# A graph layer on one core: the edge pipeline one step deeper, and the node stage's last addition at the end of its step

## The reference

```python
h = maximum(layernorm(x), 0)
em = concat([h[src], h[dst]]) @ msg_w + msg_b           # 25,000 x 256 times 256 x 128
em = relu(layer_norm(em) * msg_g + msg_beta) * edge_weight[:, None]
messages = segment_sum(em, dst) / count(dst)            # mean over the edges of each target
gate = sigmoid(h @ gate_w + gate_b)
h_new = relu(layer_norm(concat([h, messages]) @ upd_w + upd_b) * upd_g + upd_beta)
out = x + gate * h_new + (1 - gate) * h
```

## Time and profile before

| | |
|---|---|
| median of 3 runs | 1020.86 us (1020.46 to 1021.62) |
| profiled execution, its own time | 1019.86 us |
| its span | 1017.1 us |
| busy in the span | DVE 945.0 us (93%), ACT 875.1 (86%), PE 705.2 (69%), POOL 680.7 (67%) |
| mean granted clock of PE | 0.776 of full speed |
| preparation and first node groups | 0 to 40 us |
| node loop and its end | to about 480 us |
| edge steps enter | from 481.52 us |
| last output scatter of POOL | 1005.43 us |

### The profile page before, as it was taken

How to read it: one execution, slowest core, us unless ns; L and a number is a source line. 1 busy time by engine, 2 the same in 40 slices (tenths; PEclk the granted TensorE clock), 3 DMA queues, 4 the chain that set the end, 5 groups by cost and what they waited for, 6 DMA issues and landing times.

```text
span 1017.1 us, 20909 instructions
## 1 busy us (share of the span) xinstructions
PE 705.2 (69%) x3696; PEld 547.4 (54%) x3696; DVE 945.0 (93%) x4103; ACT 875.1 (86%) x3664; POOL 680.7 (67%) x602
## 2 busy tenths in 40 slices
PE   1877776777777777777477767676867676666740
PEld 1555554555555555555366556565656565555530
DVE  6999999999999999999869999998998999999990
ACT  2899999999999999999778988888788897888860
POOL 5788888888888888100344777776776777677564
PEclk9999996555555555555578998989798989999975
DMA  4255555555555455332121222221212122121110
GB/s 142 79 153 149 154 152 151 151 154 151 149 155 153 148 153 155 113 115 82 52 82 59 62 73 65 68 70 58 68 61 70 56 68 70 55 68 60 55 58 21
DMA packets 56028, 100.65 MB, mean 99 GB/s; under 512 B 13728, under 2 KB 15600, under 8 KB 55948
## 3 DMA queue, kind: packets, MB, share of 16 engines
q1 hardware_dynamic: 35766, 64.54, 17.6%
q0 software_dynamic: 18912, 34.84, 14.4%
q10 hardware_dynamic: 1270, 0.53, 0.3%
HBM read 52.34 MB, written 51.45 MB: 102 GB/s over the span
## 4 chain that ended last, share of the span: by engine, by line
DVE 56%; issue 18%; ACT 12%; PE 4%; DVEq 4%; POOL 3%; DMA 1%; ACTq 0%; SPq 0%; POOLq 0%
DVE work L430 11%; DVE st L344 9%; DVE work L441 8%; ACT junk L393 5%; DVE work L447 5%; DVE acc L441 5%; DVE acc L885 4%; PE pa L1056 3%; POOL out L557 3%; DVE mv L350 3%; DVE work L452 2%; DVEq L109 1%; DVE gt L423 1%; DVE omg L426 1%; ACT hrow L386 1%
## 5 line engine op out<-in xcount | busy, mean ns | idle before, releaser
L552 POOL DMA_INDIRECT ring<-in_x,src_i x196 | 228.7, 1167 | 175.8 <-ACT hrow L386 110.1
L552 POOL DMA_INDIRECT ring<-in_x,gidx x196 | 237.7, 1213 | 59.7 <-issue 59.7
L557 POOL DMA_INDIRECT out<-work,sidx x196 | 209.8, 1071 | 88.5 <-issue 56.9
L1056 PE MATMUL pt<-ident,hrow 128*128 128x128 f32 x588 | 143.4, 391 | 116.8 <-ACT hrow L386 108.5
L1093 PE MATMUL py<-w_u,work 128*128 128x129 f32 x784 | 203.8, 441 | 0.0
L409 ACT ACTIVATE work<-work,gt 128x128 f32<-128x128 f32 x589 | 199.6, 403 | 2.6 <-DVE work L447 2.6
L1093 PEld LDWEIGHTS py<-w_u,work 128*128 128x128 f32 x784 | 174.9, 328 | 40.4 <-issue 40.4
L1056 PEld LDWEIGHTS pt<-ident,hrow 128*128 128x128 f32 x588 | 96.6, 197 | 145.9 <-ACT hrow L386 136.6
L386 ACT ACTIVATE hrow<-xload,nb,rs 128x128 f32<-128x128 f32 x392 | 161.6, 484 | 14.4 <-DVE nb L379 7.5
L441 DVE SCALAR_TENSOR_TENSOR work<-py,rs,g_upd 128x128 f32<-128x128 f32 x588 | 163.4, 339 | 4.2 <-ACT rs L373 4.2
L393 ACT ACTIVATE junk<-py 128x128 bf16<-128x128 f32 x588 | 150.5, 266 | 8.7 <-PE py L1131 7.8
(11 more groups left out here) (151 smaller groups left out, 1543.4 us busy)
## 6 DMA issues: line engine op xcount, KB each, us to landing
xload<-in_x SPq DMA_DIRECT2D x98, 256.0 KB, 3.3
out<-work SPq DMA_DIRECT2D x98, 256.0 KB, 2.0
running_sums<-acc SPq DMA_DIRECT2D x49, 256.0 KB
ring<-in_x,src_i POOLq DMA_INDIRECT x196, 3.2
ring<-in_x,gidx POOLq DMA_INDIRECT x196, 3.2
out<-work,sidx POOLq DMA_INDIRECT x196, 2.3
w_all<-in_L_gnn_msg_w ACTq DMA_DIRECT2D x1, 128.0 KB
w_all<-in_L_gnn_upd_w ACTq DMA_DIRECT2D x1, 128.0 KB
```

Of the source, the lines that this page charges most:

```text
L552: pool.indirect_dma_start(out=dest, out_offset=None, in_=rows, in_offset=bass.IndirectOffsetOnAxis(ap=idx, axis=0), **(if_tail if rows is ...
L557: pool.indirect_dma_start(out=out, out_offset=bass.IndirectOffsetOnAxis(ap=idx, axis=0), in_=rows, in_offset=None, **if_tail).then_inc(s, 16)
L1056: last = nc.tensor.transpose(dest[:, k * H:(k + 1) * H], rows[:, k, :], ident[:, :])
```

## The change

The edge pipeline becomes one step deeper behind the running sums. On PE the transposes of the sums are those of s-5 and stand first in the step; the update matmuls are those of s-5. On ACT the copy at is that of s-5 and stands between ht_dst and the relus; post, relus and the waits belonging to them go one group further back; ht_dst waits besides for the update matmuls of the group four before, since its buffer is now still read that late. On DVE gate, mix and update normalization are those of s-7, final that of s-9, and the update normalization (with its wait for the scatter) stands behind the message normalization rather than at the step's end. In the node stage final takes the group six back and stands at the end of the step, where it took the group seven back in the middle. The edge loops run one step more, the node loop of DVE one less. REFILLED is 36 in place of 40.

PE's order, edge steps ahead of the loop, before the change: from a message matmul to the first update matmuls (pm messages, pa sums, pt h, py update).

The diff, cut to its core:

```diff
@@ -52,7 +52,7 @@
 AHEAD = 8
-REFILLED = 40
+REFILLED = 36
 EPS = 1e-5
@@ -646,9 +646,6 @@
                     minus_mean(dve, nd, s.back(1), G)
-                f = s.back(7)
-                if live(f, NG):
-                    final(dve, nc.vector, nd, f, o[:, f.at % 4])
                 if new:
@@ -669,6 +666,9 @@
                     beta(dve, nd, g, t_buf[:, g.at % 4], be_upd)
+                f = s.back(6)
+                if live(f, NG):
+                    final(dve, nc.vector, nd, f, o[:, f.at % 4])
@@ -823,7 +823,7 @@
             def edge_step(s):
-                g, m = s.back(6), s.back(4)
+                g, m = s.back(7), s.back(4)
                 fin, new, summing = live(g, EG), live(s, EG), live(m, EG)
@@ -845,7 +845,7 @@
                     minus_mean(dve, ed, s.back(1), 2 * G, -0.5)
-                f = s.back(8)
+                f = s.back(9)
                 if live(f, EG):
@@ -855,6 +855,14 @@
                     beta(dve, ed, q, acc[:, q.at % 4], be_msg, G, "beta_m", "gamma_m")
+                if fin:
+                    if beyond(g, 4):
+                        dve.wait_ge(s_scat[g.at % 4], g.rounds(16 * G))
+                    else:
+                        dve.wait_ge(s_st[g.at], 16 * len(range(g.at, NG, 4)))
+                    ed["rstd"].after(dve, s)
+                    one_mark(ed["gamma"], dve, g, by_std(t_buf[:, g.at % 4], py[:, g.at % 2], s.at % 4, 3 * G, g_upd))
+                    beta(dve, ed, g, t_buf[:, g.at % 4], be_upd)
                 if new:
@@ -867,10 +875,6 @@
                 if fin:
-                    if beyond(g, 4):
-                        dve.wait_ge(s_scat[g.at % 4], g.rounds(16 * G))
-                    else:
-                        dve.wait_ge(s_st[g.at], 16 * len(range(g.at, NG, 4)))
                     ed["gain"].after(dve, g)
@@ -895,13 +899,8 @@
                     moment(L, s, 2 * G, 2)
-                if fin:
-                    ed["rstd"].after(dve, s)
-                    one_mark(ed["gamma"], dve, g, by_std(t_buf[:, g.at % 4], py[:, g.at % 2], s.at % 4, 3 * G, g_upd))
-                if fin:
-                    beta(dve, ed, g, t_buf[:, g.at % 4], be_upd)
-
-            run_steps(dve, node_step, NG, 7, 9, 8, first=4, beside=edge_step)
+
+            run_steps(dve, node_step, NG, 6, 9, 8, first=4, beside=edge_step)
@@ -920,7 +919,7 @@
-            run_steps(dve, edge_step, EG, 8, 2 * EUN, EUN, first=7, beside=tail_step)
+            run_steps(dve, edge_step, EG, 9, 2 * EUN, EUN, first=6, beside=tail_step)
@@ -983,8 +982,8 @@
                     ed["stats"].after(act, s.back(1))
-                if live(s.back(6), EG):
-                    ed["post"].after(act, s.back(6))
+                if live(s.back(7), EG):
+                    ed["post"].after(act, s.back(7))
                 if live(s.back(3), EG):
@@ -994,11 +993,16 @@
                 if live(g, EG):
+                    if beyond(g, 4):
+                        ed["upd"].after(act, g.back(4))
                     one_mark(ed["ht"], act, g, nc.scalar.activation(ht_dst[:, (g.at + NG) % 4, :], pt[:, 1, :], ACT.Copy))
-                if live(s.back(7), EG):
-                    gated_relu(act, ed, s.back(7))
-                if live(s.back(5), EG):
-                    post(act, ed, s.back(5), (s.at + 1) % 4, 3 * G, G, 1.0)
+                g = s.back(5)
+                if live(g, EG):
+                    evacuate(ed, g, at_[:, g.at % 2, :], pa[:, :], ACT.Copy, "at", "aflip")
+                if live(s.back(8), EG):
+                    gated_relu(act, ed, s.back(8))
+                if live(s.back(6), EG):
+                    post(act, ed, s.back(6), (s.at + 1) % 4, 3 * G, G, 1.0)
                 g = s.back(1)
@@ -1008,9 +1012,6 @@
                     H_.mark(h_rows(g, h_dst[:, (g.at + NG) % XS], slot(g, 1, at), G))
-                g = s.back(4)
-                if live(g, EG):
-                    evacuate(ed, g, at_[:, g.at % 2, :], pa[:, :], ACT.Copy, "at", "aflip")
                 if live(s.back(2), EG):
@@ -1035,7 +1036,7 @@
-            run_steps(act, edge_step, EG, 7, 2 * EUN, EUN, first=6, beside=tail_step)
+            run_steps(act, edge_step, EG, 8, 2 * EUN, EUN, first=6, beside=tail_step)
@@ -1095,6 +1096,10 @@
             def edge_step(s):
+                g = s.back(5)
+                if live(g, EG):
+                    ed["sum"].after(pe, g)
+                    one_mark(ed["aflip"], pe, g, flip(pa[:, :], acc[:, g.at % 4]))
                 g = s.back(2)
@@ -1107,16 +1112,12 @@
                     one_mark(ed["msg"], pe, g, last)
-                g = s.back(4)
-                if live(g, EG):
-                    ed["sum"].after(pe, g)
-                    one_mark(ed["aflip"], pe, g, flip(pa[:, :], acc[:, g.at % 4]))
                 g = s.back(1)
...
                     one_mark(ed["flip"], pe, g, flip(pt[:, 1, :], h_dst[:, (g.at + NG) % XS]))
-                g = s.back(4)
+                g = s.back(5)
                 if live(g, EG):
@@ -1137,7 +1138,7 @@
             run_steps(pe, node_step, NG, 2, 9, 8, first=2, beside=edge_step)
-            run_steps(pe, edge_step, EG, 4, 2 * EUN, EUN, first=2)
+            run_steps(pe, edge_step, EG, 5, 2 * EUN, EUN, first=2)
```

## The result

The changed kernel takes **1113.62 us** (median of 4 runs, 1112.67 to 1114.7) beside 1021.09 us before (1020.46 to 1021.62): ratio 1.0907, 95% interval 1.0888 to 1.0926. Slower, as forecast, but by 92 us instead of 52, and outside the range (1024 to 1095).

The account below looks back on a forecast made before the run. DVE bounds the kernel now; a new edge-stage ring would take over at 10.9 us per step. 41 steps +45.1, stops +4, passage -3, end +5.7 make +51.8, 1071.7 us; with 1.0 for the median, 1073 us, range 1024 to 1095.

Parts of the forecast that it names:

- The ring: Edge stage: a new circle of waits between PE and ACT sets the step, 9.81 us at full clock against 9.52.
- Rival C: Edge stage: the new circle of waits does not bind, being under 9.4 us; 1013 us, chance 0.12.
- The clock: Edge stage: PE's 3.6 us idle time lowers its clock, adding 1.1 us per step, to 10.9 us.
- Rival B: Edge stage: PE falls to the lower clock level for good, 13.08 us per step; 1162 us, chance 0.04 with what leads to it.
- Rival A: Edge stage: the ring binds but PE's clock stays full nearly always; 1028 us, chance 0.22 including steps up to 10.3 us.
- Node stage: Node loop: moving final gains or costs nothing, as DVE has no idle time; 0, bounds -2 to +4 us.
- The passage: Between node and edge stages: DVE's 9.4 us of waits for rs shrink; 0 to -6, taken as -3 us.
- Loop stops: Edge loop: PE, without time to spare, also stops where the loop jumps back; 0 to +7.6, taken as +4 us.
- The tail: End of the kernel: everything is one step later, POOL's last scatters start after a later final; +5.7 us.
- POOL: Refill gathers over 36 groups instead of 40, 2.9 per step instead of 2.6; a slower step gives room: 0.
- The scatter wait: Edge stage: DVE's earlier update normalization waits for the scatter 1.5 us sooner, with nearly two steps of slack; 0, bounds 0 to +2.

Follow-up runs that it names:

- the edge part alone: The changed kernel with its node-stage part undone (final again in the middle of the step, group seven back): 1123.55 us, ratio 1.1026 to the kernel before.
- the node part alone: The kernel before with only the node stage's final changed, to the group six back at the step's end: 1006.11 us, ratio 0.9883.

## Why the prediction was right and wrong

- **The ring** (pa, at, relus, squares, h, pt, update matmuls): right, in its links, its waits and its size. It was 9.81 us forecast at full clock, and 9.87 measured once the clock was held. "pa <- DVE" is gone from PE's waits, and DVE waits 1.7 to 3.8 us for rs. Rival C (the ring does not bind) is excluded.
- **The clock**: this is the step that failed. Its kind was right, its size not: "A low stretch of 3 us costs 1.5 us [...] I take 1.1 us per step". Measured are 12.19 - 9.81 = 2.4 us per step. The 41 steps took 98.1 us more than before, 53 us more than the 45.1 that the sum had for them. The windows of the earlier trace rows were 2 to 3 us long because I had cut them so; I took "at least" for "about". The earlier trace rows showed one real length: after the idle time that ended at 973.52 PE was still at half clock in pa at 979.42, 5.9 us later. The ring has pt and update matmuls right behind the idle time, 3.17 us at full clock and about 6 at half, so the whole stretch lies in the ring. Rival B's sum of 13.08, which counted everything at half, was nearer to the 12.65 of the slow steps than the 10.9.
- **A misreading beside it**: "idle times of 1.89 us leave it full now" does not hold throughout. Between 540 and 960 us the kernel before has 39 idle times of 1.8 to 2.0 us ahead of pa or of the messages, and 12 of them were followed by half clock for some of the work behind them. They account for much of its 0.92. One of them:

```profile
662.96 1.06 PE L1056 MATMUL pa<-ident,acc 128*128 128x128 f32 x4 [1.89 <-DVE acc L885]
```

- The Trainium skill (TensorE: Matmul & The Clock Gate, section "HAM oscillation — how this bites in real kernels") speaks of a fall in every iteration, and the trace agrees: 0.78 over the edge loop, half clock behind each of 41 idle times. I put it down as the upper half of my range and should have made it the forecast.
- **Rival A** (clock nearly always full, 1028 us) is what the ten unused matmuls made true: 1023.4 us. That the totals are so near is in part luck. The node stage gave back 13.8 us that A did not have, and A had the rest too cheap: 41 steps took 10.5 us more than before and not 0.4, since each of three jumps of the loop makes a step of 12.2 to 12.4 us there, and the passage took 2.8 us more and not 3 less.
- **Node stage**, "0, with -2 to +4 as bounds": wrong, -14.2. "DVE has no idle time to give" was read from a busy share, and a late start can hide within that share.
- **The passage**, -3 taken, +1.4 measured. This is not the ring: the edge part alone has 61.68 us up to the eighth step, 0.6 less than before, and the node part alone 64.75, 2.5 more. Why the node part costs something there is open. **Loop stops**, +4 taken: the three steps with a jump are 12.73 us, 0.5 above the mean, 1.6 us in all; they are within the 98.1.
- **The tail**, +5.7 taken, +8.3 measured: POOL's unbroken run of scatters begins with group 43 and not 44 (answering to the earlier trace rows):

```profile
1064.66 0.69 DVE L452 TENSOR_TENSOR work<-work 128x512 f32<-128x512 f32 x1
...
1065.63 0.98 POOL L557 DMA_INDIRECT out<-work,sidx  x1 [2.69 <-DVE work L452]
```

It starts 27.8 us after the last nb instead of 24.4, and holds four scatters of 1.29 us more.
- **POOL** at 0: right; it waits for final. **The scatter wait** at 0: right in this kernel, mostly 0.45 us and once 2.2 us a step where the ring is gone.

With the 41 steps at their size and nothing else changed the sum would have been 1073 + 53 = 1126, and with the node stage's -14.2 it would have been 1112. That this is so near to 1113.6 is in part luck: the +4 for the stops is in it although the 98.1 hold them, and that makes up for more than half of the passage and the tail, which were 7 us too low together.

## What to carry to other kernels

When a change gathers an engine's short pauses into one long one, price the clock by the longest stretch at the lower level that any row shows after such a pause, from the pause's end to the first instruction at full duration. Then see which of the work behind the pause is in the critical ring. A busy share near 100% shows that an engine has no gap in its records, not that its order is free of cost: compare distances from start to start behind short instructions. Work with no use, put into the idle time itself and, as a control, into the busy time, is a cheap test of whether the clock is the cause.

## What the runs showed of the hardware

- Ten unused matmuls a step in PE's idle time made a kernel 88 us faster. In its busy time they made steps of 13.7 us, 1.5 more than the changed kernel's mean.
- Idle times of PE and the clock behind them: 1.11 to 1.19 us left it full in 38 of 38 (ten unused matmuls); 1.8 to 2.0 us were followed by half clock for some of the work in 12 of 39 (kernel before); 2.3 us left the messages at full clock and 2.5 to 2.7 us did not in the first steps with the update matmuls first; 3.34 to 3.69 us were followed by half clock in 41 of 41 (changed kernel). With five unused matmuls one of 3.21 us (1136.57) still left it full, so the length alone does not settle it.
- In the node loop the granted clock's record does not fit the durations. At 400 us it is 0.50 before and 1.00 after the change, and the same eight records take the same time. Their bias matmuls take 0.61 us in both, as in the edge loop at half clock (0.39 at full). Before, then after:

```profile
401.25 2.09 PE L1093 MATMUL py<-w_u,work 128*128 128x129 f32 x8
```

```profile
403.30 2.09 PE L1094 MATMUL py<-w_u,work 128*128 128x129 f32 x8
```

So durations are the safer reading.
- On DVE final starts 0.21 us after the start of nb, where statistics start 0.07 us after it. Behind an instruction that takes 0.6 us from start to start it costs nothing extra.
- Two chips took 1.4 ms for kernels that take 1.02 elsewhere. PE stood still there in waits of the kind "issue", in the node loop's first steps above all (five unused matmuls, 60 to 360 us):

```profile
PE pt L1057 <- issue: 221.1, 7, 35.5
```

Why is open.
